# First-layer weights of the first batch, mixed and applied by halves of the outputs on two engines

## The reference, cut to what matters

```python
masked_w = weight * mask[None, :, :]                 # (8, 256, 256)
w_bot = jnp.einsum('bg,got->bot', y, masked_w)       # one matrix per batch
x = x + jnp.einsum('bnt,bot->bno', x, w_bot) + bias
# second layer, for the shared weights and the 2 best of 8 experts:
g = x @ gate_w;  u = x @ up_w
out += w_e * ((gelu(g) * u) @ down_w)
x = x + out
```

## Time and profile before

| what | us |
|---|---|
| median of three runs | 414.45 |
| lowest, highest | 414.2, 414.62 |
| the profiled execution | 414.13 |
| its span | 412.3 |
| PE busy (share) | 407.1 (99%) |
| DVE busy | 305.4 (74%) |
| ACT busy | 253.1 (61%) |
| POOL busy | 313.3 (76%) |

### The profile page before, as it was taken

One profiled execution on the slowest core, in us unless ns is written; L12 is line 12 of the kernel. 1 busy time (PEld: TensorE's weight loads), 2 busy tenths in 40 slices (PEclk: granted clock), 3 DMA queues, 4 the chain that ended last, 5 costly groups with the idle time before them and its releaser, 6 DMA issues.

```text
span 412.3 us, 7445 instructions
## 1 busy us (share of the span) xinstructions
PE 407.1 (99%) x2241; PEld 354.9 (86%) x2241; DVE 305.4 (74%) x511; ACT 253.1 (61%) x484; POOL 313.3 (76%) x322
## 2 busy tenths in 40 slices
PE   8999999999999999999999999999999999999997
PEld 6778888888988888888888888988888889888886
DVE  4787897586768887866777879866687677677784
ACT  6586767675555568655555567757555557675541
POOL 1699999999709679999634879999680986999730
PEclk9999999999999999999999999999999999999999
DMA  8552443333100522243000253222300042232201
GB/s 266 201 171 77 135 122 78 101 90 103 43 24 2 166 89 79 90 142 102 28 25 2 49 180 102 76 76 82 96 25 25 0 129 76 76 111 72 51 0 53
DMA packets 19616, 35.23 MB, mean 85 GB/s; under 512 B 2179, under 2 KB 2947, under 8 KB 19587
## 3 DMA queue, kind: packets, MB, share of 16 engines
q1 hardware_dynamic: 19296, 34.61, 27.3%
q10 hardware_dynamic: 290, 0.26, 0.2%
HBM read 32.77 MB, written 2.10 MB: 85 GB/s over the span
## 4 chain that ended last, share of the span: by engine, by line
PE 96%; DVE 1%; ACT 1%; issue 0%; POOL 0%; DVEq 0%; POOLq 0%
PE o_ps L549 16%; PE p_ps L549 12%; PE g_ps L495 10%; PE g_ps L494 10%; PE g_ps L498 10%; PE u_ps L495 10%; PE u_ps L494 10%; PE u_ps L498 10%; PE l_ps L450 2%; PE g_ps L620 1%; PE u_ps L413 1%; PE p_ps L431 0%; PE o_ps L589 0%; DVE u_ps L985 0%; DVE out_sb L1067 0%
## 5 line engine op out<-in xcount | busy, mean ns | idle before, releaser
L1166 POOL TENSOR_TENSOR eg_lo<-raw_g,eg_hi 128x512 fp32r<-128x512 f32 x64 | 88.5, 1404 | 11.2 <-ACT eg_hi L691 11.2
L720 ACT ACTIVATE gelu<-g_ps 128x512 f32<-128x512 f32 x95 | 57.0, 600 | 57.5 <-PE g_ps L498 56.2
L990 DVE SCALAR_TENSOR_TENSOR u_ps<-gelu,route_cur,u_ps 128x512 f32<-128x512 f32 x64 | 48.1, 751 | 52.4 <-PE u_ps L498 49.8
L1026 DVE TENSOR_TENSOR h_lo<-t_raw,h_hi 128x1024 fp32r<-128x1024 f32 x46 | 80.9, 1759 | 0.2 <-ACT h_hi L753 0.2
L740 ACT CAST h_hi<-u_ps 128x256 fp32r<-128x256 f32 x46 | 17.2, 373 | 60.1 <-DVE t_raw L1005 42.8
L1208 POOL TENSOR_TENSOR ed_lo<-s_raw,ed_hi 128x512 fp32r<-128x512 f32 x30 | 52.7, 1757 | 0.0
L495 PE MATMUL g_ps<-x_hi,eg_lo 128*128 128x512 f32 (+1 forms) x128 | 50.3, 393 | 0.0
L1206 POOL TENSOR_TENSOR ed_lo<-raw_d,ed_hi 128x384 fp32r<-128x384 f32 x30 | 39.4, 1313 | 14.3 <-ACT ed_hi L700 14.1
L494 PE MATMUL g_ps<-x_hi,eg_hi 128*128 128x512 f32 (+1 forms) x128 | 50.1, 391 | 0.0
L495 PE MATMUL u_ps<-x_hi,eg_lo 128*128 128x512 f32 (+1 forms) x128 | 49.8, 389 | 0.0
L494 PE MATMUL u_ps<-x_hi,eg_hi 128*128 128x512 f32 (+1 forms) x128 | 49.8, 389 | 0.0
(11 more groups left out here) (226 smaller groups left out, 1154.3 us busy)
## 6 DMA issues: line engine op xcount, KB each, us to landing
raw_g<-experts SPq DMA_DIRECT2D x64, 256.0 KB, 2.8
raw_d<-experts SPq DMA_DIRECT2D x32, 256.0 KB, 2.7
l_raw<-l_w SPq DMA_DIRECT2D x8, 256.0 KB, 5.1
x_in<-xT SPq DMA_DIRECT2D x8, 256.0 KB, 4.0
raw_g<-shared SPq DMA_DIRECT2D x8, 256.0 KB, 4.2
outT<-out_sb SPq DMA_DIRECT2D x6, 256.0 KB, 3.3
raw_d<-shared SPq DMA_DIRECT2D x4, 256.0 KB, 2.9
mask<-l_mask SPq DMA_DIRECT2D x2, 128.5 KB, 5.5
```

What stands on the lines that cost most here:

```text
L720: act.activation(gelu[:, s % 2], l0_ps if at_first(b) and s == 1 else g_ps, ACT.Gelu_apprx_tanh).then_inc(gelu_done, 1)
L990: dve.scalar_tensor_tensor(u_ps[:, s % 2], gelu[:, s % 2], route_cur[:, k:k + 1], u_ps[:, s % 2], ALU.mult, ALU.mult).then_inc(h_done, 1)
L1026: dve.tensor_tensor(h_lo[:, at], t_raw[:], h_hi[:, at].bitcast(F32), ALU.subtract).then_inc(t_lo_done, 1)
L1166: pool.tensor_tensor(eg_lo[:, j % RING], raw_g[:, j % RAW_G], eg_hi[:, j % RING].bitcast(F32), ALU.subtract).then_inc(gu_lo_done, 1)
```

## The change

The weights are stored by halves of the outputs and groups of four (`QUAD`). The loads go in the order half 0 g 0 to 3 (512 KB), x whole (512 KB), half 0 g 4 to 7 (512 KB), mask and bias in one (257 KB), half 1 g 0 to 3 (512 KB), half 1 g 4 and 5, half 1 g 6 and 7 (256 KB each); then the shared weights as before.

Each half is now mixed by both engines. Half 0: g 0, 1, 4, 5 on DVE, g 2, 3, 6, 7 on PE. Half 1: g 0, 1, 4, 6 on DVE, g 2, 3, 5, 7 on PE. DVE adds the two sums (`add_mixed_0`; for half 1 two adds of 128 columns), masks (half 1 in two parts of 128 columns), and makes the low parts; ACT's casts of half 1 are two of 128 columns too. ACT makes five diagonals where it made eight. PE runs six `keep_warm` matmuls where it ran eleven. Half 1 waits on DVE until half 0 is masked. The low parts of x go from DVE to POOL, ahead of its other work. In ACT's order `first_x1_hi(0)` stands ahead of the up half of chunk 0, the cast of shared chunk 3 ahead of `activate(0, 0)`, the cast of the first block sums behind `split_b2`. In POOL's order the low parts of the shared chunks come ahead of the first block sums, and in steps 3 and 5 one chunk comes ahead of the sums. In `first_gate_up` both high parts of a half come ahead of both low parts. In the other batches the same eight mixing steps read the new layout.

The core of the diff:

```diff
-WARM_UP = 5
+WARM_UP = 3
+QUAD = 4
...
-            for g in range(2):
-                load_l0(g)
-            load_x_half(0, 0)
-            for g in range(2, 4):
-                load_l0(g)
-            load_x_half(0, 1)
-            for g in range(4, G):
-                load_l0(g)
-            for oh in range(HH):
-                sp.dma_start(mask[:, oh], l0_mask[oh]).then_inc(mask_in[oh], 16)
+            load_l0(0, 0)
+            load_x_0()
+            load_l0(0, 1)
+            sp.dma_start(mask[:], l0_mask).then_inc(mask_in, 16)
+            load_l0(1, 0)
+            for i in range(2):
+                load_l0_last(i)
             shared_weights()
             batch_0()
...
-            def mix_l0(g):
-
-                pe.wait_ge(diag_done, g + 1)
-                pe.wait_ge(l0_in[g], 16)
-                mm = pe.matmul(mix_ps, diag[:, g], l0_raw[:, g, D:2 * D], start=(g == 0), stop=(g == G - 1))
-                if g == G - 1:
+            def mix_l0(oh, g, first=False, last=False):
+
+                pe.wait_ge(diag_done, DIAGS.index(g) + 1)
+                pe.wait_ge(l0_in[l0_load(oh, g)], 16)
+                mm = pe.matmul(mix_ps[oh], diag[:, g], l0_raw[:, oh, g], start=first, stop=last)
+                if last:
                     mm.then_inc(mixed, 1)
 
-            def pass_x():
+            def pass_x(hh):
                 pe.wait_ge(ident_r_done, 1)
-                for hh in range(HH):
-                    pe.wait_ge(x_hi_done, hh + 1)
-                    pe.matmul(p_ps[:, hh], ident_r, x_hi[:, hh], start=True, stop=False)
-                    pe.wait_ge(x_lo_done, hh + 1)
-                    pe.matmul(p_ps[:, hh], ident_r, x_lo[:, hh], start=False, stop=False)
+                pe.wait_ge(x_hi_done, hh + 1)
+                pe.matmul(p_ps[:, hh], ident_r, x_hi[:, hh], start=True, stop=False)
+
+            def pass_x_rest(hh):
+                pe.wait_ge(x_lo_done, hh + 1)
+                pe.matmul(p_ps[:, hh], ident_r, x_lo[:, hh], start=False, stop=False)
+
+            def first_layer_part(w, oh, th, x, last=False):
+                at = oh * D + th * P
+                mm = pe.matmul(p_ps[:, oh], w[:, at:at + P], x[:, th], start=False, stop=last)
+                if last:
+                    mm.then_inc(l0_done, 1)
 
             def first_layer_0():
-                for oh in range(HH):
-                    pe.wait_ge(l0_hi_done, oh + 1)
+
+                pe.wait_ge(first_hi_done, 1)
+                for th in range(HH):
+                    first_layer_part(l0_hi, 0, th, x_hi)
+                mix_l0(1, 5)
+                mix_l0(1, 7, last=True)
+                for th in range(HH):
+                    first_layer_part(l0_hi, 0, th, x_lo)
+                pe.wait_ge(first_lo_done, 1)
+                for th in range(HH):
+                    first_layer_part(l0_lo, 0, th, x_hi, last=(th == HH - 1))
+                for th in range(HH):
+                    pe.wait_ge(first_hi_done, 2 + th)
                     for x in (x_hi, x_lo):
-                        for th in range(HH):
-                            at = oh * D + th * P
-                            pe.matmul(p_ps[:, oh], l0_hi[:, at:at + P], x[:, th], start=False, stop=False)
-                    pe.wait_ge(l0_lo_done, oh + 1)
-                    for th in range(HH):
-                        at = oh * D + th * P
-                        mm = pe.matmul(p_ps[:, oh], l0_lo[:, at:at + P], x_hi[:, th], start=False, stop=(th == HH - 1))
-                    mm.then_inc(l0_done, 1)
+                        first_layer_part(l0_hi, 1, th, x)
+                for th in range(HH):
+                    pe.wait_ge(first_lo_done, 2 + th)
+                    first_layer_part(l0_lo, 1, th, x_hi, last=(th == HH - 1))
 
             def first_layer(b, oh):
 
                 if oh == 0:
-                    pe.wait_ge(l0_hi_done, HH * b + HH)
-                    pe.wait_ge(l0_lo_done, HH * b + HH)
+                    pe.wait_ge(l0_hi_done, HH * b)
+                    pe.wait_ge(l0_lo_done, HH * b)
                     pe.wait_ge(x_hi_done, HH * b + HH)
                     pe.wait_ge(x_lo_done, HH * b + HH)
                 else:
...
-                    for ps, off, hi_done, lo_done in ((g_ps, GATE, part_hi_done, part_lo_done), (u_ps[:, 0], UP, gu_hi_done, gu_lo_done)):
+                    for ps, off, hi_done in ((g_ps, GATE, part_hi_done), (u_ps[:, 0], UP, gu_hi_done)):
                         at = off + hh * P
                         pe.wait_ge(hi_done, 1)
                         pe.matmul(ps, w_hi[:, at:at + P], x1_at(x1_hi, 0, hh), start=(hh == 0), stop=False)
+                    for ps, off, lo_done in ((g_ps, GATE, part_lo_done), (u_ps[:, 0], UP, gu_lo_done)):
+                        at = off + hh * P
                         pe.wait_ge(lo_done, 1)
                         pe.matmul(ps, w_lo[:, at:at + P], x1_at(x1_hi, 0, hh), start=False, stop=False)
...
-            for g in range(G):
-                if g == G - 2:
-                    pass_x()
-                mix_l0(g)
-                if g < G // 2:
-                    keep_warm(1)
+            mix_l0(0, 2, first=True)
+            mix_l0(0, 3)
+            pass_x(0)
+            keep_warm(1)
+            pass_x(1)
+            mix_l0(0, 6)
+            mix_l0(0, 7, last=True)
+            pass_x_rest(0)
+            mix_l0(1, 2, first=True)
+            mix_l0(1, 3)
+            pass_x_rest(1)
             first_layer_0()
...
-            def split_l0_0(oh):
-                act.wait_ge(masked, oh + 1)
-                act.copy(l0_hi[:, oh * D:(oh + 1) * D], l0_first[:, oh * D:(oh + 1) * D]).then_inc(l0_hi_done, 1)
+            def split_l0_0():
+                act.wait_ge(first_masked, 1)
+                act.copy(l0_hi[:, 0:D], l0_first[:, 0:D]).then_inc(first_hi_done, 1)
...
-            for g in range(2):
+            for g in DIAGS[0:2]:
                 scale_ident(g)
             act.wait_ge(routed, ROUTED_SHIFTED)
             act.activation(exps[:], shifted[:], ACT.Exp).then_inc(exp_done, 1)
-            for g in range(2, G):
+            for g in DIAGS[2:]:
                 scale_ident(g)
             for hh in range(HH):
                 split_x(0, hh)
             act.activation(gelu[:, 0, 0:8], shifted[:, 0], ACT.Gelu_apprx_tanh)
-            for oh in range(HH):
-                split_l0_0(oh)
+            split_l0_0()
+            for th in range(HH):
+                split_l0_1(th)
             split_gate(0)
+            first_x1_hi(0)
             split_up(0)
-            first_x1_hi(0)
             split_gate(1)
             first_x1_hi(1)
             split_up(1)
             split_gate(2)
             split_up(2)
+            split_shared(FIRST)
+            activate(0, 0)
             split_shared_d(0)
-            activate(0, 0)
-            split_shared_s(0)
             copy_b12(0, 0)
-            weights_beside(0, 0)
             activate(0, 1)
             split_b11(0, 0)
             split_b2(0, 0)
+            split_shared_s(0)
             first_x1(0)
             weights_beside(0, 1)
...
-            def combine_0(g):
-                dve.wait_ge(l0_in[g], 16)
-                acc, w = half(l0_first, 0), l0_raw[:, g, 0:D]
-                if g == 0:
-                    dve.tensor_scalar(acc, w, cond_all[:, 0, g:g + 1], None, ALU.mult).then_inc(combined, 1)
+            def combine_0(oh, g, first=False):
+                dve.wait_ge(l0_in[l0_load(oh, g)], 16)
+                acc, w = half(l0_first, oh), l0_raw[:, oh, g]
+                if first:
+                    dve.tensor_scalar(acc, w, cond_all[:, 0, g:g + 1], None, ALU.mult).then_inc(first_mixed, 1)
                 else:
-                    dve.wait_ge(combined, g)
-                    dve.scalar_tensor_tensor(acc, w, cond_all[:, 0, g:g + 1], acc, ALU.mult, ALU.add).then_inc(combined, 1)
-
-            def apply_mask_0(oh):
-                dve.wait_ge(mask_in[oh], 16)
-                if oh == 0:
-                    dve.wait_ge(combined, G)
-                    mix = half(l0_first, 0)
-                else:
-                    dve.wait_ge(mixed, 1)
-                    mix = mix_ps
-                dve.tensor_tensor(half(l0_first, oh), mix, mask[:, oh, 0:D], ALU.mult).then_inc(masked, 1)
-
-            def split_l0_0(oh):
-                dve.wait_ge(l0_hi_done, oh + 1)
-                dve.tensor_tensor(half(l0_lo, oh), half(l0_first, oh), half(l0_hi, oh).bitcast(F32), ALU.subtract).then_inc(l0_lo_done, 1)
-
-            def first_x_lo(hh):
-                dve.wait_ge(x_hi_done, hh + 1)
-                dve.tensor_tensor(x_lo[:, hh], x_in[:, hh], x_hi[:, hh].bitcast(F32), ALU.subtract).then_inc(x_lo_done, 1)
+                    dve.wait_ge(first_mixed, 4 * oh + {1: 1, 4: 2, 5: 3, 6: 3}[g])
+                    dve.scalar_tensor_tensor(acc, w, cond_all[:, 0, g:g + 1], acc, ALU.mult, ALU.add).then_inc(first_mixed, 1)
+
+            def add_mixed_0():
```

(65 more changed lines are left out.)

58 lines of the change are left out of this document (39 added, 19 removed).

## The result

| | before | after |
|---|---|---|
| median of 19 runs each, us | 414.38 | 415.18 |
| profiled execution, us | 414.13 | 415.01 |
| its span, us | 412.3 | 413.3 |

The ratio is 1.0018 [1.0012, 1.0025]: slower by 0.8 us, which is within the 0.2% that I take as the limit of what a measurement tells from no change. The direction was the forecast one. The size was not: +0.8 in the medians and +0.9 in the profiled executions, where I had +2.05.

A forecast was written before the change was run, and what follows sets the result against it. PE's unbroken work from 26 us was taken as the bound, begun by step 3's gate product behind `activate(0, 2)`. First product +1.9, then +0.15, gave +2.05: 416.2 us profiled, 416.5 median; range 414.6 to 417.5.

The forecast's parts named there:

- the sum up to `first_x1_hi(1)`: Loads, mixing, mask and casts ahead of this ACT instruction: it would start at 17.6 us, against 16.05 before.
- the mask of half 0: DVE's masking of the first mixed half: begins at 11.1 us, against 11.81 before.
- the adds of half 1: DVE's adding of both engines' sums: begins at about 14.8 us, released by PE's mixes.
- the stretch behind x1: From `first_x1_hi(1)` at 17.6 us to PE's gate product of step 3 at 27.4; before, 16.05 and 25.39.
- Its way of reading: PE is busy from 26 to 404 us, so what moves `activate(0, 2)` moves the end by as much.
- Landing of x: Loads at the start: x whole at 7.0 us, from equal amounts landing at equal times, nothing gained for larger transfers.
- the rival "faster": Early PE rate and no hole in the loads, mask of half 0 before about 9.0: 413.6 us, chance 0.11.
- PE's rate: Matmuls rise from half to full rate at 13.0 us, after 5.4 us of unbroken feed from 7.6.
- Mixing: Mixing by halves on DVE and PE: PE's mixes end at 14.5 us, later than DVE's combines at 14.2.
- the four 128-column steps: DVE's dependent steps on half 1: 0.3 us each, 1.1 in all, bounds 0.2 less and 0.6 more.
- The move of that chunk: POOL's low part of a shared chunk ahead of the block sums: gives more cover, no cost on the path.
- First product to `activate(0, 2)`: From DVE's first product to this ACT instruction: 5.0 us before, 0.15 later with the casts exchanged.

The follow-up runs named there:

- `a_best`: Changed kernel with low parts of x on DVE, route weighing behind step 3, and ACT's gelu of step 2 directly behind `split_b2`; median 414.87 us, ratio 1.0018.
- `a_old_orders`: Changed kernel with the orders of ACT, POOL and `first_gate_up` behind the first layer as before; median 414.94 us, ratio 1.0025.
- `a_loads_256`: Changed kernel with each 512 KB load issued as two of 256 KB in the same order of bytes; ratio 1.0048.
- `a_cold`: Changed kernel without its six warm-up matmuls on zeros; median 415.35 us, ratio 1.0031.
- `a_best2`: Changed kernel with x's low parts on DVE, route weighing behind step 3, gelus of steps 2 and 3 and shared chunk 5 moved earlier; 414.62 us, ratio 1.0013.
- `a_xlo_dve`: Changed kernel with the low parts of x made on DVE again instead of POOL; ratio 1.0010.
- `b_x_whole`: Kernel before the change with x loaded by one transfer of 512 KB instead of two halves; ratio 1.0012.
- `a_pool_order`: Changed kernel with POOL's block sums and low part of shared chunk 3 back in the old order behind the first layer; ratio 1.0018.

## Why the prediction was half right

The direction was right and the size wrong, by two errors of opposite sign. The step that failed first is the sum up to `first_x1_hi(1)`: I had it at 17.6, it was 15.96. Of these 1.64 us, 0.94 lie ahead of the mask of half 0 (10.16 for 11.1: x at 5.54 for 7.0, and PE's rise at 7.4 for 13.0). Another 0.76 lie between that mask and the adds of half 1, where at the early rate PE's mixes were no longer the later of the two (from the adds on it took 0.06 more than forecast). The step that was missing is the wait of DVE for POOL. With ACT's cast of the block sums it made the stretch behind x1 1.02 longer, where I had 0.46. That the time lies in the stated range is luck as far as these two offset each other.

Its way of reading held for this change: it acts through the gate product of step 3 (+0.93 there, +1.0 in the span; 386.9 and 387.0 us lie behind it), and PE's 378 us stayed full but for 0.3. It did not hold as a rule: in `a_best` the same product came earlier and the end did not follow, and in `a_old_orders` 387.7 us lie behind it. `first_x1_hi(1)` was no longer released by PE, as forecast. The terms one by one:

1. Landing of x, 7.0: it was 5.54, the term that was most off. I took equal amounts at equal times, and nothing for larger pieces, though the hole of the earlier trace rows lay open. With 512 KB pieces the slice moved 389 GB/s, with 256 KB ones in the same order 252 (`a_loads_256`), before 207. I had named this under the rival "faster".
2. PE's rate, rise at 13.0: it was 7.4. I had carried the one profile's stretch of unbroken feed over to this kernel. Two profiles of the identical kernel have 9.8 and 9.3, and kernels with zeros matmuls anything from 6.5 to 9.8, `a_loads_256` 13.1. `a_cold` shows in one profile that a late rise has a price: rise at 13.9, gate product +1.64. "TensorE: Matmul & The Clock Gate", Part 1, of the Trainium skill says of itself that the moment varies from run to run with one kernel; the traces agree.
3. Mixing: mask of half 0 at 11.1, was 10.16; adds of half 1 at 14.8 released by PE, were at 13.10 and behind DVE's own combines (1.66 for three, as predicted); the four 128-column steps 1.1 in all and 0.29 each, as taken. So `first_x1_hi(1)` at 15.96, not 17.6. The rival "faster" put its point of decision at a mask of half 0 before 9.0. Of its two conditions the landing was there (5.54); the rise came at 7.4, a microsecond behind its 6.4. It missed that point by 1.2, of which at most 1.07 is the combine that POOL held.
4. The hold-up of DVE by POOL stood nowhere in my text. It cost 1.07 at the combine, and 1.02 more than before over the last three routing steps (1.45 in all before, 2.47 after). In the kernel before, POOL had no rests of x at the start, and its chunk 3 came behind the block sums; its shorter instructions held two of the three steps there as well. The move of that chunk I had checked for what waits on POOL, not for what runs beside it.
5. First product to `activate(0, 2)`: 5.15 predicted, 5.02 measured. Yet the term is not understood by that: the block-sum cast in it costs 0.51 (3.40 against 2.89), in place of 0.15, and the way from the first to the second product was 0.5 shorter (1.62 against 2.14). I take it that the hold-up ahead of the first had used up the second's wait for its gelu (0.60 before, none after); that is argued and not tested.

Summed against the predicted kernel: up to x1 1.64 less (15.96 for 17.6); behind it a loss of 1.02 where I had 0.46 (27.4 less 17.6, against 9.34). That is 27.4 - 1.64 + 0.56 = 26.32, the measured moment. Against the kernel before: the orders behind x1 cost 0.85 to 1.02 in the stretch, and what the loads and the mixing by halves gave ahead of it the runs don't fix. `first_x1_hi(1)` lies at 15.55 to 16.51 in four executions with the old mixing and loads (mean 16.10). With the new ones and the rests of x on POOL it lies at 15.58 to 16.23 in five (mean 16.00), so the x that landed 1.7 earlier gave almost nothing. With the rests of x on DVE it lies at 14.82 to 16.11 in six (mean 15.51). That would be a gain of 0.6, but `a_best` and `a_best2` were profiled in the fastest of their executions. Among these six it is earliest where PE's rate rose earliest (14.82 with the rise at 6.5) and latest where that rose at 9.0 and 9.7 (16.09 and 16.11). There, in `a_xlo_dve`, DVE waited 0.58 for the load and 0.69 for PE's mixes in place of POOL. `a_cold` and `a_loads_256`, with their late rise, and `b_x_whole`, with other loads (16.99), are in none of the three groups.

## What to carry to other kernels

When an instruction is moved to another engine or place, look at what runs beside it on the engine that shares its way to memory, not only at what waits for it. A gain in front of a chain of several engines is worth only what the next in line leaves: here 1.38 behind x1 became 0.05 (`a_pool_order`), and only six moves together took the whole loss back, in one profile. A moment of a single profile, such as that of PE's rate, is one sample; forecast with both ends.
